# A graph network on one core: another order of masks, last rows and products where the mean begins

## What is computed

```python
h = relu(layernorm(x));  outs = [h];  mask = adj > 0
for i in range(2):                               # two attention layers on 8192 x 8192 masks
    Wh = g @ W[i]                                # g = h in the first, the last h in the second
    e = leaky_relu(u + v.T + c);  att = softmax(where(mask, e, -9e15), axis=1)
    g = 0.2 * h + 0.8 * elu(att @ Wh);  outs.append(g)
x = x + concat(outs) @ mlp_w + mlp_b
h3 = relu(layernorm(x));  a = (adj == 1)
out = x + concat([a @ h3 / deg, h3]) @ weight + bias
```

## Time and profile before

| | us |
|---|---|
| median of 3 runs | 1729.23 |
| lowest, highest | 1729.03, 1730.32 |
| the profiled execution: its own time | 1730.36 |
| its span (first to last instruction in the profile) | 1728.6 |
| TensorE busy, share of the span | 1557.8, 90% |
| VectorE busy, share | 1509.0, 87% |
| ScalarE busy, share | 1298.6, 75% |
| layer two ends, the mean begins (first L1978) | 1470.71 |

### The profile page before, as it was taken

The page is one execution under the profiler, slowest core; times in us unless marked ns, Lnnn a source line. Parts: engine busy times, 40 slices in busy tenths (PEclk is TensorE's granted clock), DMA queues, the critical chain, the costliest instruction groups (busy, mean ns, idle before and its releaser), DMA issues. The chain is left out here.

```text
span 1728.6 us, 50394 instructions
## 1 busy us (share of the span) xinstructions
PE 1557.8 (90%) x21853; PEld 1507.8 (87%) x21853; DVE 1509.0 (87%) x2448; ACT 1298.6 (75%) x1488; POOL 81.7 (5%) x118
## 2 busy tenths in 40 slices
PE   2477898989898988889789999999999999899999
PEld 2377888888798888888789999999999999799999
DVE  7899999999999999999799877879688788866665
ACT  3777899999899898998689999999999996200000
POOL 1100000101010010101000000000000000000000
PEclk9589999999999999999889999999999999999999
DMA  7988999999999999997121212122121211023231
GB/s 272 358 311 311 379 383 399 355 411 384 411 368 402 383 388 410 366 408 276 56 51 44 62 39 62 39 69 62 39 63 38 63 33 50 2 78 91 86 94 45
DMA packets 112397, 351.82 MB, mean 204 GB/s; under 512 B 8720, under 2 KB 16944, under 8 KB 112176
## 3 DMA queue, kind: packets, MB, share of 16 engines
q1 hardware_dynamic: 88736, 300.07, 45.9%
q0 software_dynamic: 8960, 29.43, 6.0%
q10 hardware_dynamic: 14480, 19.11, 3.0%
HBM read 321.26 MB, written 27.33 MB: 202 GB/s over the span
## 5 line engine op out<-in xcount | busy, mean ns | idle before, releaser
L505 ACT ACTIVATE region<-ub,bigv 128x1024 uint8<-128x1024 f32 x1024 | 1096.2, 1150 | 28.7 <-PE bank L1750 11.3
L1744 PE MATMUL bank<-wsplit,region 128*128 128x195 bf16 x8192 | 786.9, 250 | 33.5 <-DVE region L977 29.4
L1744 PEld LDWEIGHTS bank<-wsplit,region 128*128 128x128 fp8e3 x8192 | 695.4, 99 | 48.7 <-DVE region L977 23.7
L1750 PE MATMUL bank<-wsplit,region 128*128 128x130 f16 x8192 | 558.0, 221 | 39.9 <-DVE region L987 38.8
L1750 PEld LDWEIGHTS bank<-wsplit,region 128*128 128x128 fp8e3 x8192 | 503.4, 98 | 56.9 <-DVE region L987 53.1
L987 DVE SCALAR_TENSOR_TENSOR region<-region 128x512 uint32<-128x512 uint32 x512 | 338.8, 681 | 9.2 <-PE bank L1750 8.4
L977 DVE SCALAR_TENSOR_TENSOR region<-region 128x512 uint32<-128x512 uint32 x512 | 334.3, 682 | 8.3 <-ACT region L505 8.2
L1005 DVE TENSOR_SCALAR region<-region 128x4096 uint8<-128x4096 int32 x128 | 292.2, 2283 | 4.9 <-DMA region<-in_adj 4.7
L1978 PE MATMUL bank<-wsplit,region 128*128 128x129 f16 x4032 | 237.9, 221 | 7.0 <-DVE region L1550 7.0
L1978 PEld LDWEIGHTS bank<-wsplit,region 128*128 128x128 fp8e3 x4032 | 236.2, 98 | 8.0 <-DVE region L1550 8.0
L1550 DVE TENSOR_SCALAR region<-region 128x512 uint32<-128x512 uint32 x256 | 100.9, 424 | 47.9 <-PE bank L1978 43.1
(11 more groups left out here) (240 smaller groups left out, 727.3 us busy)
## 6 DMA issues: line engine op xcount, KB each, us to landing
region<-in_adj SPq DMA_DIRECT2D x128, 2048.0 KB, 11.7
region<-codes_d SPq DMA_DIRECT2D x112, 256.0 KB, 2.6
codes_d<-region ACTq DMA_DIRECT2D x64, 256.0 KB, 6.7
ub<-u_d POOLq DMA_DIRECT2D x16, 512.0 KB, 7.8
hg<-h_d POOLq DMA_DIRECT2D x16, 256.0 KB, 7.1
stg<-m_d POOLq DMA_DIRECT2D x16, 256.0 KB, 4.9
region<-in_x SPq DMA_DIRECT2D x4, 512.0 KB, 6.7
h_d<-wsplit POOLq DMA_DIRECT2D x4, 512.0 KB, 4.3
```

Source lines behind the costliest of these rows:

```text
L505: last = nc.scalar.activation(sv[:, b, :], ub[G % 2][:, :], ACT.Relu, bias=bigv[l][:, t:t + 1], scale=BIG)
L1744: return nc.tensor.matmul(acc_on[it], columns(onb[U % NS], it, b), wsplit[:, c * TC + 2 * q + b, 0:WC], start=(c == 0 and q == 0 and b == ...
L1750: return nc.tensor.matmul(acc_off[it], columns(offb[U % NO], it, b), woff[:, c * TC + 2 * q + b, WO:WO + WF], start=(c == 0 and q == 0 and ...
```

## The change

In the loop of layer two, `degree_weights` and `split_y(0)`, `split_y(1)` are done at the end of tile 61 (`NT - 3`) instead of 62, `split_y(2)` and `split_y(3)` in tile 62 instead of 63, and tile 63 does `split_y(4)`, which was done in the mean's beginning by `scaled_y(4)`, `cast_y(4)` and `low_y(4)`. In the mean's beginning VectorE makes a second pair of masks and the squares and variances of group 6 before `sums_out`, the roots and normal rows of group 6 come sooner, `base(5)` and `base(6)` too; TensorE does half tile 1 before the second product of group 5, and the turn of h3(6) after half tile 4 instead of 6, its products before half tile 6 instead of 8; ScalarE takes the high part and the turned copy of group 6 earlier.

```diff
--- before.py
+++ after.py
@@ -651,7 +651,7 @@
                                          pb[:, :].rearrange("p (t s c) -> p t s c", s=2, c=C)[:, :, 0, :], ACT.Copy, scale=winv).then_inc(q_out, 1)
 
                 def cast_y(c):
-                    act.wait_ge(ys_a, c - 3)
+                    act.wait_ge(ys_a, c - 4)
                     nc.scalar.activation(wf16[:, grp(c), 0:C], yb, ACT.Copy).then_inc(ys_h, 1)
 
                 def high_last_h3(e):
@@ -665,13 +665,12 @@
                     nc.scalar.activation(hcat[0][:, :, 0:C], hb[(NG + e) % 2][:, :, :], ACT.Copy, scale=hq[:, 1, 0:1]).then_inc(hi2_r, 1)
 
                 take_last_h3(5)
-                cast_y(4)
                 take_y(5, 0, tpb)
+                high_last_h3(6)
                 take_y(5, 1, tpb)
+                take_last_h3(6)
                 cast_y(5)
                 row_exp(2 * NG - 1)
-                high_last_h3(6)
-                take_last_h3(6)
                 high_last_h2(7)
                 take_y(6, 0, tpb)
                 take_y(6, 1, bank[6])
@@ -1417,7 +1416,7 @@
                     nc.vector.tensor_tensor(yb, hw[:, grp(c), 0:C], wide(ymul[:, grp(c)]), ALU.mult).then_inc(ys_a, 1)
 
                 def low_y(c):
-                    dve.wait_ge(ys_h, c - 3)
+                    dve.wait_ge(ys_h, c - 4)
                     nc.vector.tensor_tensor(wf16[:, grp(c), C:2 * C], yb, wf16[:, grp(c), 0:C], ALU.subtract).then_inc(w_y, 1)
 
                 for n in range(NT):
@@ -1514,15 +1513,16 @@
                             normal_2(g - 2)
                         if r == 4:
                             high_3(g - 2)
-                    if n == NT - 2:
-                        old_x(7)
-                    if n == NT - 2:
+                    if n == NT - 3:
                         degree_weights()
                         split_y(0)
                         split_y(1)
-                    if n == NT - 1:
+                    if n == NT - 2:
+                        old_x(7)
                         split_y(2)
                         split_y(3)
+                    if n == NT - 1:
+                        split_y(4)
 
                 def mix(i):
                     M = 2 * NT + i - NX
@@ -1557,67 +1557,68 @@
                         mix(i + 1)
 
                 pick_half(0)
+                pick_half(1)
+                squared(6)
+                variances(6)
                 sums_out(NG + 7)
-                pick_half(1)
+                pick_half(2)
                 row_scales(NG + 7)
-                scaled_y(4)
                 x_and_y(5, 0, tpb)
+                pick_half(3)
                 lonely_add(NG + 7)
-                low_y(4)
-                pick_half(2)
                 lonely(NG + 7)
-                squared(6)
+                roots(6)
+                pick_half(4)
+                normal_2(6)
                 x_and_y(5, 1, tpb)
                 lonely_mean(NG + 7)
-                pick_half(3)
-                variances(6)
+                pick_half(5)
+                low_3(6)
+                lonely_add(NG + 7)
+                denominators(NG + 7)
+                pick_half(6)
                 scaled_y(5)
-                lonely_add(NG + 7)
-                pick_half(4)
+                attend(NG + 7)
+                pick_half(7)
                 low_y(5)
-                roots(6)
-                denominators(NG + 7)
-                pick_half(5)
-                attend(NG + 7)
-                normal_2(6)
-                pick_half(6)
-                low_3(6)
+                pick_half(8)
                 elu(NG + 7)
                 residual(NG + 7)
-                pick_half(7)
+                pick_half(9)
                 x_and_y(6, 0, tpb)
                 x_and_y(6, 1, bank[6])
                 low_2(7)
-                pick_half(8)
                 scaled_y(6)
-                pick_half(9)
+                pick_half(10)
                 low_y(6)
+                pick_half(11)
+                base(5)
+                pick_half(12)
+                base(6)
                 new_x(7)
                 means(7)
-                pick_half(10)
                 centred(7)
                 squared(7)
-                pick_half(11)
+                pick_half(13)
                 variances(7)
                 roots(7)
-                pick_half(12)
+                pick_half(14)
                 normal_2(7)
-                pick_half(13)
+                pick_half(15)
                 low_3(7)
-                pick_half(14)
-                pick_half(15)
                 pick_half(16)
                 pick_half(17)
+                pick_half(18)
                 x_and_y(7, 0, tpb)
                 x_and_y(7, 1, bank[6])
-                pick_half(18)
+                pick_half(19)
                 scaled_y(7)
-                pick_half(19)
+                pick_half(20)
                 low_y(7)
-                for s in range(20, 24):
-                    pick_half(s)
-                    if s > 20:
-                        base(s - 16)
+                pick_half(21)
+                base(7)
+                pick_half(22)
+                pick_half(23)
 
                 def mean_sums(g):
                     b = fin[g % 2]
@@ -1994,17 +1995,19 @@
                 claim_b7()
                 multiply_h3(5, 0, tpb)
                 mean_half(0)
+                mean_half(1)
                 claim_b7()
                 multiply_h3(5, 1, tpb)
-                for s in range(1, 7):
+                for s in range(2, 5):
                     mean_half(s)
                 claim_b7()
                 transpose_h3(6)
-                mean_half(7)
+                mean_half(5)
                 claim_b7()
                 multiply_h3(6, 0, tpb)
                 multiply_h3(6, 1, bank[6])
-                mean_half(8)
+                for s in range(6, 9):
+                    mean_half(s)
                 claim_b7()
                 transpose_h2(7, tpb)
                 mean_half(9)
```

## The result

| | before | after |
|---|---|---|
| median, 6 runs each (us) | 1729.78 | 1719.22 |
| lowest, highest | 1727.0, 1732.13 | 1717.5, 1721.97 |
| ratio, 95% interval | | 0.9939, 0.9929 to 0.995 |
| profiled execution, its span | 1728.6 | 1716.6 |
| **tail**: last tile of layer two to the end (see below) | 262.9 | 253.6 |

What follows compares the result with a forecast made beforehand. VectorE's instruction list was taken to bound the mean's beginning, TensorE its steady part. Layer two 0, mean's beginning 9.1 us less, steady part 0: from the median 1729.23 to 1720.1 us, range 1718.4 to 1723.6.

Steps and rivals of the forecast that it cites:

- The bound and its cost: Mean's beginning: VectorE's instruction list sets the pace from 1470.8 to 1506; TensorE loses 10.6 us, the most to gain.
- parts 1 to 3: Layer two: moved degree weights and splits (4.3 us) hidden, hole 4.30 to 1.3; VectorE 2.2 us sooner at first mask pair.
- Without this cover 4.3 us would come in: End of layer two: unhidden, degree weights and two splits add 4.3 us before the sums; mean begins that much later.
- Part 4: Ahead of the sums: second mask pair, square, variance of group 6 cost nothing; sums end at 1470.8; 3.1 us freed.
- The walk: Mean's beginning, new lists stepped with trace times: half tile 16 at 1506.1 for 1515.2; waits of 0.2, 0.7, 0.5 us.
- 9.1 expected: Mean's beginning: half tile 16 starts 9.1 us sooner; layer two and the steady part 0.
- The clock did not fall: Rival, mean's beginning: clock falls behind the remaining waits, uncovered, costing 1.65 us; 1721.8 us; chance 0.14.
- the slower chain: Rival, VectorE's group 7 steps before pair 14: 0.6 to 0.7 us more each, 3 us; 1723.1 us; chance 0.13.
- the ring: Rival "slower", mean's beginning: six to eight handovers in a row at 1.9 us cost 10.8 to 14.4; 1734.5 us; chance 0.05.
- Nothing is gained: Rival: something later (code loads, bases, sums at 1541) sets the mean's end, gain given back; 1729.2 us; chance 0.06.

Runs made afterwards that it cites:

- clock_kept: The kernel before with 16 to 32 identity matmuls in each of five TensorE waits; tail 262.9 us, against 262.9 before.
- splits_only: The kernel before with the new places of the splits and no scaled, cast and low y of group 4 in the mean; tail 261.6 us.
- late_splits: The kernel after with degree weights and splits 0 and 1 back in tile 62, splits 2, 3 and 4 in tile 63; tail 257.7 us.

## Why the prediction was right

**The bound and its cost.** Right. 10.6 us lost in the old beginning, VectorE's list as the bound: in the old order TensorE at full clock didn't end sooner (clock_kept), while two operations less on VectorE gave 1.3 us (splits_only); in the new order a doubled operation came out whole. What is left of the 10.6 is the 1.4 us of waits below.

**Layer two, parts 1 to 3.** Right. 4.33 us of degree weights and splits for 4.3, the hole 1.26 for 1.3, TensorE without a wait up to the mean, layer two unchanged. "Without this cover 4.3 us would come in": late_splits gave 4.1. The words behind it, that the mean would begin that much later, were wrong: it began 2.7 us later (7.7 behind the tail's start for 5.0), for its first unit needs only the third reduction. The rest of the 4.1 went by as half clock (1.55, less 0.1 of waiting at the turn of h3(6)); the sum is VectorE's.

**Part 4.** Right, within 0.3 us: from the last tile's first on matmul, the first mask at -1.2 (expected 1464.8 less 1465.7, -0.9), the sums' end at 5.1 as before. Moved back behind the sums, the work cost 1.8 of its 1.9.

**The walk.** It gave 35.4 us from the mean's first matmul to half tile 16; measured 35.3. Waits by starts: 0.27 ahead of the turn of h3(6) (0.2 expected), 0.5 for pair 14 (0.7), 0.65 for the turn of h3(7) (0.5): some 1.4 in all, as walked.

**The size.** 9.1 expected, 9.3 in the tail. The medians show 10.6 (8.6 to 12.3 by the interval); the rest over 9.3 is scatter of the first layer, as far as the profiles show, and the interval holds 9.3. The prediction's range has a slip at its high end: 1723.1 and 0.2 make 1723.3, not 1723.6; the measured 1719.22 lies inside either.

**The rivals.** The clock did not fall behind the two waits that are left, so what a fall there would have cost stays unmeasured. Table of stretches after, with the granted clock 1.00, 1490 to 1505 us, and the steady part:

```profile
1490.00:1505.00 15.00, 14.15 (x243) 13.83 (x241) 13.28 (x38) 2.58 (x4) 0.74 (x2) 1.00 0.10 38
1540.00:1710.00 170.00, 170.00 (x2926) 170.00 (x2924) 114.17 (x267) 0.00 (x0) 3.21 (x5) 1.00 0.29 83
```

It did fall behind a wait of 2.53 us in late_splits, where the loss was covered. The waits alone don't tell when: behind a row of waits like that of the kernel before it stayed up in splits_only. VectorE's chain ran as walked: behind the sums it waited for no other engine up to 1502 us. A released matmul of the mean started 0.06 us behind its mask (mask from 1497.11 in 0.42 us, matmul at 1497.59), a turn 0.15 behind its low part (1500.10, low part done at 1499.95), so neither the slower chain nor the ring came. "Nothing is gained" is refuted by the steady part: busy for 170.00 of 170.00 us as before.

## What to carry to other kernels

Where the bound engine waits at the start of a steady stage, list what the other engine's instructions cost in order and walk both lists with the trace's own steps; the tails came within 0.3 us of what was expected in every run but one, a slip about one wait included; only the sum of brackets was 0.5 off. Here work was free only in a wait: in tile 61 and ahead of the sums it cost nothing, a tile later the same work cost 4 us. A loss that the profile shows (half clock for 3.3 us in the kernel before, and again in late_splits) counts only if nothing else would have waited there anyway: ask how late the bounding engine is by itself before you put a price on it.

## What was not expected of the hardware

The clock fell in one execution and not in another that ran nearly the same instructions. From 815 to 820 us it was 0.66 in the one and 1.00 in the other, behind waits of TensorE of 2.02 and 1.18 us. Near 1502 us the kernel before fell to 0.50 for 3.3 us and splits_only did not, both behind a wait of 1.90 us with four waits of 1 to 1.75 us ahead of it. What decides it stays open. The point between the layers moved by 6.2 us over 13 profiles, while the 601 us of layer two behind it moved by 0.5. And half clock cost nothing both times that it fell in the mean's beginning, 1.4 and 1.55 us of slower matmuls, for VectorE was later still; for the kernel before runs show it, for late_splits it is read from the rows.
